# Weighted sums of three-block attention steps issued in one stretch of three blocks instead of two stretches

## The chip, the cores and the metric

The kernel runs on one core of one Trainium2 chip. The metric is the device time of one execution in microseconds (us). Its engines are PE (TensorE), DVE (VectorE), ACT (ScalarE), POOL (GpSimd) and SP (SyncE); each works through its own instructions in order, and they meet in semaphores.

## The reference

On x of 4 sequences of 1024 tokens and width 256, three layers run one after another: a mixture of experts, an attention, and the same mixture again.

```python
x = L0_attn_x
x = x + 0.5 * _L0_ffn_ref(_layernorm(x, axis=-1), Wg, W_in, W_out)
x = x + _L0_attn_ref(_layernorm(x, axis=-1), Wq, bq, Wk, bk, Wv, bv, Wo, bo, J_attn, lambda_attn)
x = x + 0.5 * _L0_ffn_ref(_layernorm(x, axis=-1), Wg, W_in, W_out)
```

The change lies in the attention alone, of 16 heads with 16 values each:

```python
scores = jnp.einsum('bhid,bhjd->bhij', Q, K) / scale
QJ = jnp.einsum('bhid,hde->bhie', jnp.tanh(Q), J_attn)
delta = jnp.einsum('bhie,bhje->bhij', QJ, jnp.tanh(K))
scores = scores + lambda_attn * delta
causal = jnp.triu(jnp.ones((S, S), dtype=bool), k=1)
scores = jnp.where(causal, -jnp.inf, scores)
probs = jax.nn.softmax(scores, axis=-1)
out = jnp.einsum('bhij,bhjd->bhid', probs, V)
```

## The kernel before

The attention takes 16 groups g of four heads (4 sequences by 4 groups of heads). Queries and keys are packed so that one product over 96 rows gives the whole score. For each query the kernel first needs the greatest score (the maximum pass, for a head that is more than one group ahead), then the exponentials of the scores less that maximum, then the weighted sums of the values.

**Six steps a group, four heads a step.** `STEPS` (line 1604) cuts the keys and queries of a group into six steps s. A step holds one to three blocks; a block is one tile of 128 keys against up to 512 queries. Step 0 has three blocks on the diagonal (512, 128 and 384 queries wide), step 1 one (256), steps 2 and 3 two full ones (512 each), step 4 three (512, 128, 384), step 5 one (256). For step s and head j, q = 4 s + j. In each q, PE forms the scores of one head of one step (`score`, line 2213) into one of two tiles `s_ps`, and ACT takes their exponential into `wts` (line 2089). The score of q needs the exponential of q - 2, which frees the tile.

**Masking on POOL.** Blocks on the diagonal have the weights above it set to zero by POOL (line 1913) after ACT has done all four heads of the step: three instructions for a three-block step, one for a one-block step, each for all four heads. PE waits for them on the semaphore `cleared`.

**Weighted sums.** `mix` (line 2225) multiplies the weights of a block by the values of its 128 keys. A product has 17 output rows (16 values and the sum of the weights), and the four heads go to four strips of the output tile `o_ps`, 32 partitions apart, so that four products use four strips of the array at once. The profile counts two matmuls for each such product: a block is 8 matmuls of the form `128*17`, in two sets of four. The sums of step s - 1 are issued among the scores of step s; those of step 5 at the end of the group. In `body` (line 2243), `when` (line 2256) says behind which heads j of step s they go: for a two-block step one block behind j = 1 and one behind j = 3; for a three-block step the first block behind j = 2 and the other two behind j = 3. The three-block steps are 0 and 4, so that concerns q = 6 and 7 (s = 1) and q = 22 and 23 (s = 5) of each group.

**The maximum pass, fitted in between.** In each q PE also issues two "maximum" units (`max_unit`, line 2177) of later heads: one ahead of the score of q, one behind it. A unit is one tile of 128 queries against up to 512 keys, written to one of three PSUM banks `m_ps`; DVE takes its maximum (lines 1964 and 1967). The twelve units of a head (`UNITS`, line 1608) are named here by query tile and half of the keys, as (6, 1). After the last, DVE folds them (line 1971), PE turns the result (`turn`, line 2193), ACT negates it (line 2032) and sends it to the packed queries. In the first ten groups (the hosts) PE also fits in the projections of later tokens, each into one of the same three banks: "x" transposes, "y" a product of six 512-wide matmuls for queries or keys, "v" one of six 256-wide matmuls for values. Of a host group, "y" comes at q = 5 and q = 6 (behind `mix`), and in groups with even numbers "v" at q = 21 and q = 23. In the last group, output tiles (line 295) take that place for q below 16.

**The order** is written out: `ORDER` and the assignment of banks (line 1712) are computed ahead from the units and projections alone. Before each one PE waits until the reader of the bank's earlier content is done (`free_bank`, line 2118). The bank of unit (7, 1), for instance, is in most groups the one that (5, 1) had. PE takes nothing past such a wait.

```python
when = {1: (3,), 2: (1, 3), 3: (2, 3)}[len(blocks)]
part = {j_: blocks[n:n + 1] if n + 1 < len(when) else blocks[n:] for n, j_ in enumerate(when)}.get(j)
if part:
    mix(g, u, s - 1, part, j == 3)
```

Of the kernel before, what the change touches and what calls it, by code (L numbers as in the profile page):

```python
# [1590 lines left out]
def attend(kit, c, proj, sum_dram, packs, v_dram, o_dram, inv_dram, wo_dram, bo_dram, group, group_in):  # L1591
# [18 lines left out]
    with ExitStack() as ctx:  # L1610
# [56 lines left out]
        def events(g, q):  # L1667

            first = PER_GROUP * (g + 1) + LEAD + sum(SHARE[:q])
            at = lambda units: after_units[min(units, len(after_units) - 1)]  # L1670
            return EVENTS[at(first):at(first + SHARE[q])]
# [16 lines left out]
        def project_at(g, q):  # L1688

            if g == GROUPS - 1:  # L1690
                return [("o", q)] if q < IN_ATTENTION else []
            what = IN_GROUP[g % 2].get(q) if 0 <= g < HOSTS else None
            return [what[:1] + (half_in(g),) + what[1:]] if what else []
# [418 lines left out]
        def tensor(pe):  # L2112
# [82 lines left out]
            def ahead(some):  # L2195
                for event in some:
                    if kind(event) == "turn":
                        turn(*event[:2])
                    elif kind(event) == "max":
                        max_unit(*event)  # L2200
                    else:
                        projected(event)
# [10 lines left out]
            def score(g, u, s, j):  # L2213
                ch, blocks = STEPS[s]
                q = s * GH + j
                if s == 0:
                    pe.wait_ge(row_in[j], (g + 1) * 16)
                pe.wait_ge(weighed, g * NS * GH + q + 1)
                for kt, col, q0, w, lead in blocks:
                    at = ch * QC + q0  # L2220
                    last = nc.tensor.matmul(s_ps[q % 2][:, col - lead:col + w], kp[u][:, j, kt * P:(kt + 1) * P],  # L2221
                                            qp[u][:, j, at - lead:at + w], start=True, stop=True)
                last.then_inc(scored, 1)

            def mix(g, u, s, blocks, done):

                ch = STEPS[s][0]
                if (g, s) == (0, 0):
                    pe.wait_ge(loaded[0], 16)
                for kt, col, q0, w, lead in blocks:  # L2230
                    if kt == 0:
                        pe.wait_ge(o_taken, 1 + g * 2 + ch)
                    if kt // 4 == ch:
                        pe.wait_ge(cleared, g * clears[NS] + clears[s + 1])
                    for j in range(GH):
                        pe.wait_ge(weighed, 2 + g * NS * GH + s * GH + j + 1)
                        last = nc.tensor.matmul(o_ps[j * HP:j * HP + HV, q0:q0 + w], vg[u][:, kt, j, :],  # L2237
                                                wts[(u * NS + s) % 2][:, j, col:col + w], start=(kt == 0),
                                                stop=(kt == ch * 4 + 2), skip_group_check=True)
                if done:  # L2240
                    last.then_inc(mixed, 1)

            def body(g, u):
                if g == 1:
                    pe.wait_ge(made, 2)
                for s in range(NS):
                    for j in range(GH):
                        q = s * GH + j
                        to_come = events(g, q)
                        ahead(to_come[:1])  # L2250
                        score(g, u, s, j)
                        ahead(to_come[1:2])
                        if s:

                            blocks = STEPS[s - 1][1]
                            when = {1: (3,), 2: (1, 3), 3: (2, 3)}[len(blocks)]
                            part = {j_: blocks[n:n + 1] if n + 1 < len(when) else blocks[n:] for n, j_ in enumerate(when)}.get(j)
                            if part:
                                mix(g, u, s - 1, part, j == 3)
                        ahead(to_come[2:])  # L2260
                        ahead(project_at(g, q))
                mix(g, u, NS - 1, STEPS[NS - 1][1], True)
# [3 lines left out]
            for event in LENT:  # L2266
                was_read(event)
            groups(body)

        functions = {"sync": sync, "gpsimd": gpsimd, "vector": vector, "scalar": scalar, "tensor": tensor}  # L2270
# [123 lines left out]
```

## Time and profile before

| | us |
|---|---|
| median of 3 runs | 1597.59 |
| lowest and highest run | 1595.5, 1605.68 |
| span of the profiled execution, first to last instruction | 1576.1 |
| PE busy | 1439.2 (91%) |
| DVE busy | 1022.7 (65%) |
| ACT busy | 712.3 (45%) |
| POOL busy | 684.3 (43%) |

The profile gives the span of its execution, and no time of its own beside it; the median is 21.5 us above that span. Mean granted TensorE clock over the span is 0.961 of full speed. The groups of the attention begin with their first score at 548.53 us and end at 1144.9 us; a group with an even number takes 41.3 us while it hosts projections, one with an odd number 37.4 to 37.5 us, and those from the tenth on about 32.1 us.

How to read the rows: times are us from the start of the span; a row of the timeline gives start, duration, engine, line, operation, tiles and count, and in brackets how long the engine was idle before it and what ended that. Matmuls overlap, so what one costs is the distance from its start to the start of the next, not its duration.

### The profile page before, as it was taken

How to read it: one execution, taken by the hardware profiler on the slowest of the kernel's cores; microseconds unless marked ns; L12 is line 12 of the kernel's file. 1: busy time of each engine (PE TensorE's matmuls, PEld its weight loads, DVE VectorE, ACT ScalarE, POOL GpSimd, SP SyncE). 2: the span in 40 equal slices, each digit the busy share in tenths (PEclk: the TensorE clock that was granted, in tenths of full speed). 3: DMA queues.
4: the chain of work that ended last, by engine and by line, in shares of the span. 5: the costliest groups of instructions: out<-in, count | busy, mean ns of one | idle time of the engine just before them, and what ended most of it. 6: DMA issues, size and time to landing. Idle time of an engine off the chain costs nothing. (4 is left out here: it accounts for less than half of the span.)

```text
span 1576.1 us, 25755 instructions
## 1 busy us (share of the span) xinstructions
PE 1439.2 (91%) x8992; PEld 1095.1 (69%) x8992; DVE 1022.7 (65%) x2609; ACT 712.3 (45%) x1117; POOL 684.3 (43%) x650
## 2 busy tenths in 40 slices
PE   4699999999877599999999999999986999999998
PEld 3589988989765355555555555555555888989997
DVE  7855665655386677776777778887367566565554
ACT  5333333333232156666666666666563333333332
POOL 1375556564524433333333331323403655656643
PEclk9799999999988699999999999999987999999999
DMA  9444443442378926666666668672064444345422
GB/s 307 131 106 98 94 88 64 92 101 28 67 216 201 316 76 169 168 169 169 169 168 169 154 169 242 161 218 100 29 204 148 101 96 87 67 94 101 93 37 25
DMA packets 125720, 208.61 MB, mean 132 GB/s; under 512 B 24424, under 2 KB 86376, under 8 KB 122536
## 3 DMA queue, kind: packets, MB, share of 16 engines
q1 hardware_dynamic: 88984, 160.06, 35.3%
q0 software_dynamic: 30720, 38.46, 14.9%
q10 hardware_dynamic: 5904, 8.66, 1.9%
q8 instruction: 63, 1.03, 0.3%
q14 instruction: 49, 0.40, 0.1%
HBM read 126.36 MB, written 84.64 MB: 134 GB/s over the span
## 5 line engine op out<-in xcount | busy, mean ns | idle before, releaser
L2089 ACT ACTIVATE a_wts<-a_s_psum 128x1024 f32<-128x1024 f32 (+1 forms) x384 | 301.0, 809 | 183.9 <-PE a_s_psum L2221 181.9
L1964 DVE CUSTOM_DVE_ANT_0 a_m_psum<-a_m_psum,mask 128x128 f32<-128x128 f32 (+1 forms) x492 | 238.7, 501 | 130.2 <-PE a_m_psum L2187 122.5
L2187 PE MATMUL a_m_psum<-a_kp,a_qp 96*128 96x512 f32 (+2 forms) x737 | 272.2, 398 | 20.5 <-DVE a_parts L1964 6.5
L2187 PEld LDWEIGHTS a_m_psum<-a_kp,a_qp 96*128 96x128 f32 x737 | 140.0, 192 | 130.1 <-DVE a_parts L1964 52.5
L1913 POOL TENSOR_SCALAR_AFFINE_SELECT a_wts<-a_wts 128x512 f32<-128x512 f32 x128 | 78.4, 637 | 328.0 <-ACT a_wts L2089 328.0
L1032 ACT ACTIVATE e_act_a<-e_a_psum 128x512 f32<-128x512 f32 (+1 forms) x192 | 101.2, 527 | 259.9 <-PE e_a_psum L1109 259.9
L2221 PE MATMUL a_s_psum<-a_qp,a_kp 97*128 97x512 f32 (+2 forms) x768 | 210.6, 356 | 0.4
L243 POOL DMA_INDIRECT e_slots<-normalized,e_token x160 | 168.7, 1054 | 81.7 <-issue 47.2
L949 DVE TENSOR_TENSOR e_hid<-e_act_a,e_g_psum 128x512 f32<-128x512 f32 (+1 forms) x192 | 114.5, 596 | 131.8 <-PE e_g_psum L1109 127.5
L1128 PE MATMUL e_o_psum<-e_w_hi,e_h_hi 128*128 128x256 f32 x640 | 183.2, 286 | 0.0
L890 POOL DMA_INDIRECT out<-e_res,e_sum_row x80 | 126.5, 1581 | 126.6 <-ACT e_res L1044 113.5
L890 POOL DMA_INDIRECT sums<-e_res,e_sum_row x80 | 126.5, 1581 | 126.1 <-ACT e_res L1044 105.2
L1128 PE MATMUL e_o_psum<-e_w_hi,e_h_lo 128*128 128x256 f32 x640 | 181.0, 283 | 0.0
L1128 PE MATMUL e_o_psum<-e_w_lo,e_h_hi 128*128 128x256 f32 x640 | 181.0, 283 | 0.0
L1967 DVE TENSOR_REDUCE a_parts<-a_m_psum 128x1 f32<-128x512 f32 x245 | 168.7, 689 | 8.5 <-PE a_m_psum L2187 6.2
L2237 PE MATMUL a_o_psum<-a_wts,a_vg 128*17 128x512 f32 (+3 forms) x1536 | 156.7, 496 | 4.3 <-POOL a_wts L1913 2.7
L2221 PEld LDWEIGHTS a_s_psum<-a_qp,a_kp 97*128 97x128 f32 x768 | 133.8, 192 | 18.4 <-ACT a_wts L2089 4.9
L1109 PE MATMUL e_a_psum<-e_s_hi,e_w_hi 128*128 128x512 f32 (+1 forms) x384 | 139.2, 363 | 5.4 <-DVE e_s_lo L929 2.8
L1044 ACT ACTIVATE e_res<-e_o_psum,e_gate 128x256 f32<-128x256 f32 x160 | 76.0, 475 | 147.3 <-PE e_o_psum L1128 147.3
L1109 PE MATMUL e_a_psum<-e_s_lo,e_w_hi 128*128 128x512 f32 (+1 forms) x384 | 136.0, 354 | 0.0
L1109 PE MATMUL e_a_psum<-e_s_hi,e_w_lo 128*128 128x512 f32 (+1 forms) x384 | 136.0, 354 | 0.0
L1109 PE MATMUL e_g_psum<-e_s_hi,e_w_hi 128*128 128x512 f32 (+1 forms) x384 | 135.9, 354 | 0.0
(292 smaller groups left out, 2757.3 us busy)
## 6 DMA issues: line engine op xcount, KB each, us to landing
packs<-x_res SPq DMA_DIRECT2D x48, 512.0 KB, 5.9
e_w_raw<-in_W_in SPq DMA_DIRECT2D x16, 1024.0 KB, 6.7
a_qp<-packs SPq DMA_DIRECT2D x15, 1024.0 KB, 8.1
a_kp<-packs SPq DMA_DIRECT2D x15, 1024.0 KB, 14.0
e_w_raw<-in_W_out SPq DMA_DIRECT2D x16, 512.0 KB, 8.6
normalized<-r_xn SPq DMA_DIRECT2D x16, 512.0 KB, 4.6
packs<-q_pack SPq DMA_DIRECT2D x16, 512.0 KB, 6.8
a_qp<-packs SPq DMA_DIRECT2D x16, 512.0 KB, 10.1
```

Of the source, the lines that this page charges most:

```text
L243: pool.indirect_dma_start(held["slots"][e % 2][:, j * ROW:(j + 1) * ROW], None, xn_dram, bass.IndirectOffsetOnAxis(ap=held["token"][:, at: ...
L890: nc.gpsimd.indirect_dma_start(sum_dram, bass.IndirectOffsetOnAxis(ap=sum_row[:, at:at + 1], axis=0), res[j][:], None, bounds_check=last_r ...
L949: nc.vector.tensor_tensor(hid[q][:, 0:n], act_a[q][:, 0:n], g_ps[q][:, 0:n], ALU.mult).then_inc(hid_done, 1)
L1032: nc.scalar.activation(act_a[q][:, 0:n], a_ps[q][:, 0:n], ACT.Gelu).then_inc(gelu_done, 1)
L1109: last = nc.tensor.matmul(bank[q][:, 0:n], w_in_at(w, k, half + f), s[:, k, c0:c0 + n], start=(z == 0), stop=(z == len(terms) - 1))
L1128: last = nc.tensor.matmul(o_ps[(u * ST + c0 // P + j) % 2][:, 0:D], s[:, k, j * P:(j + 1) * P], w_out_at(w, k), start=(z == 0), stop=(z == ...
L1964: nc.vector.tensor_tensor_reduce(products, products, c["mask"][:, QC - width:], 1.0, MASKED, ALU.add, ALU.max, top).then_inc(max_read, 1)
L1967: nc.vector.reduce_max(top, products, AX.X).then_inc(max_read, 1)
L2089: nc.scalar.activation(wts[(u * NS + s) % 2][:, j, 0:w], s_ps[q % 2][:, 0:w], ACT.Exp).then_inc(weighed, 1)
L2187: nc.tensor.matmul(m_ps[bank((n, h, z))][:, 0:stream], qp[n % NB][0:PACK, h, qt * P:(qt + 1) * P], kp[n % NB][0:PACK, h, part * QC:part * ...
L2221: last = nc.tensor.matmul(s_ps[q % 2][:, col - lead:col + w], kp[u][:, j, kt * P:(kt + 1) * P], qp[u][:, j, at - lead:at + w], start=True, ...
L2237: last = nc.tensor.matmul(o_ps[j * HP:j * HP + HV, q0:q0 + w], vg[u][:, kt, j, :], wts[(u * NS + s) % 2][:, j, col:col + w], start=(kt == ...
```

## The change

In `body` of the attention's tensor program, the entry for three blocks in `when` becomes `(3,)`. All three blocks of steps 0 and 4 are then issued behind head j = 3 of the next step; behind j = 2 there is none.

```diff
-                            when = {1: (3,), 2: (1, 3), 3: (2, 3)}[len(blocks)]
+                            when = {1: (3,), 2: (1, 3), 3: (3,)}[len(blocks)]
```

## Rows read from the trace of the kernel before

**Rows 1.** The page's costliest groups: the weighted sums.
```profile
L2237 PE MATMUL a_o_psum<-a_wts,a_vg 128*17 128x512 f32 (+3 forms) x1536 | 156.7, 496 | 4.3 <-POOL a_wts L1913 2.7
```

**Rows 2.** Busy time by window, one group each: 2, 4 and 11; the eighth number is the clock.
```profile
core 0: us, PE busy (x) PEld busy (x) DVE busy (x) ACT busy (x) POOL busy (x), PEclk, DMA share, GB/s
630.12:671.43 41.31, 38.95 (x239) 22.70 (x238) 29.23 (x90) 24.75 (x38) 14.03 (x18) 1.00 0.62 161
...
708.92:751.91 42.99, 40.61 (x239) 23.25 (x238) 29.21 (x89) 24.76 (x38) 14.02 (x18) 0.96 0.61 155
...
979.09:1011.24 32.15, 31.26 (x198) 17.10 (x197) 25.98 (x85) 20.44 (x31) 9.62 (x10) 1.00 0.57 157
```

**Rows 3.** Timeline of PE, q = 6 and 7 of host group 6.
```profile
799.60 0.40 PE L2187 MATMUL a_m_psum<-a_kp,a_qp 96*128 96x512 f32 x1
799.93 1.05 PE L2237 MATMUL a_o_psum<-a_wts,a_vg 128*17 128x512 f32 x8
800.92 0.50 PE L2143 MATMUL a_m_psum<-a_x_hi,q_w_hi 128*128 128x512 f32 x1
801.25 0.39 PE L2143 MATMUL a_m_psum<-a_x_lo,q_w_hi 128*128 128x512 f32 x1
801.48 0.40 PE L2143 MATMUL a_m_psum<-a_x_hi,q_w_lo 128*128 128x512 f32 x1
...
802.98 1.06 PE L2237 MATMUL a_o_psum<-a_wts,a_vg 128*17 128x128 f32 x16
```

**Rows 4.** Timeline of DVE there: the end of reading unit (0, 0).
```profile
800.04 0.14 DVE L1964 DVE_READ_ACCUMULATOR2_ANT a_parts<- 128x1 f32 x1
```

**Rows 5.** Timeline of PE, q = 6 and 7 of group 11.
```profile
985.38 0.49 PE L2187 MATMUL a_m_psum<-a_kp,a_qp 96*128 96x512 f32 x1
986.07 1.05 PE L2237 MATMUL a_o_psum<-a_wts,a_vg 128*17 128x512 f32 x8 [0.20 <-issue]
...
987.72 1.06 PE L2237 MATMUL a_o_psum<-a_wts,a_vg 128*17 128x128 f32 x16
988.70 0.27 PE L2193 MATMUL a_m_psum<-ident,a_tops 128*8 128x128 f32 x1
```

**Rows 6.** Timeline of DVE there: ends of reading (6, 1) and (0, 0).
```profile
985.18 0.14 DVE L1964 DVE_READ_ACCUMULATOR2_ANT a_parts<- 128x1 f32 x1
...
986.61 0.14 DVE L1964 DVE_READ_ACCUMULATOR2_ANT a_parts<- 128x1 f32 x1
```

**Rows 7.** Timeline of PE, q = 22, q = 23 and the group's end, even host group 6.
```profile
826.03 1.05 PE L2237 MATMUL a_o_psum<-a_wts,a_vg 128*17 128x512 f32 x8
...
827.74 1.06 PE L2237 MATMUL a_o_psum<-a_wts,a_vg 128*17 128x128 f32 x16
...
829.63 0.63 PE L2237 MATMUL a_o_psum<-a_wts,a_vg 128*17 128x256 f32 x8
830.18 0.39 PE L2187 MATMUL a_m_psum<-a_kp,a_qp 96*128 96x256 f32 x1
```

**Rows 8.** Timeline of DVE there: reading (5, 1), then (7, 0).
```profile
826.42 0.14 DVE L1964 DVE_READ_ACCUMULATOR2_ANT a_parts<- 128x1 f32 x1
826.42 0.69 DVE L1967 TENSOR_REDUCE a_parts<-a_m_psum 128x1 f32<-128x512 f32 x1
```

**Rows 9.** Timeline of PE, the end of odd host group 7.
```profile
865.91 1.74 PE L2237 MATMUL a_o_psum<-a_wts,a_vg 128*17 128x128 f32 x24
867.58 0.38 PE L2187 MATMUL a_m_psum<-a_kp,a_qp 96*128 96x256 f32 x1
```

**Rows 10.** Timeline of DVE there: reading (6, 0), then the end of (5, 1).
```profile
863.57 0.69 DVE L1967 TENSOR_REDUCE a_parts<-a_m_psum 128x1 f32<-128x512 f32 x1
...
864.51 0.14 DVE L1964 DVE_READ_ACCUMULATOR2_ANT a_parts<- 128x1 f32 x1
```

**Rows 11.** Timeline of PE, q = 22 and the group's end, group 14.
```profile
1104.47 1.05 PE L2237 MATMUL a_o_psum<-a_wts,a_vg 128*17 128x512 f32 x8 [1.20 <-POOL a_wts L1913]
...
1107.11 0.62 PE L2237 MATMUL a_o_psum<-a_wts,a_vg 128*17 128x256 f32 x8 [0.29 <-POOL a_wts L1913]
```

## The prediction

> **What bounds the kernel now.** I read the list of costliest groups first, then busy time by window, then the timelines of PE and DVE around q = 6, 7, 22 and 23. The weighted sums take 156.7 us of PE and are hardly waited for: 4.3 us in 1536 matmuls [rows 1]. PE is busy in 31.26 of 32.15 us of a late group, DVE in 25.98, ACT in 20.44 [rows 2]. So PE sets the time, and an attention of 16 groups would gain from whatever makes PE's stream shorter. But DVE, at 81%, runs close behind, and PE reaches it only through three banks. Where PE issues several units with little between them it waits for DVE; a block of weighted sums is the time in which DVE catches up. The change takes one such block from between the units of q = 6 and 7 (and 22 and 23) and puts it behind them all. So the question at each of the 32 places (16 groups, two each) is what PE meets once that block is gone.
>
> **Prices, from starts to starts.** A 512-wide matmul among others like it costs 0.23 (801.25 to 801.48) [rows 3]. From the last unit to the sums it is 0.33 (799.60 to 799.93): going in costs 0.10. A stretch of one 512-wide block takes 0.99 (799.93 to 800.92) [rows 3], one of a 256-wide block 0.55 (829.63 to 830.18) [rows 7]; so 256 columns cost 0.44, and 0.11 is paid once, at the end. The two blocks of 128 and 384 take 0.98 together (987.72 to 988.70) [rows 5]: the number of blocks costs nothing, their columns do. Behind the stretch the first matmul costs 0.33 instead of 0.23 (800.92 to 801.25) [rows 3], another 0.10. One stretch less therefore saves 0.10 + 0.11 + 0.10 = 0.31 us of PE, and 32 of them 9.9 us. The first block, moved into the later stretch, costs 0.88 there.
>
> That PE pays for going in and out is what the rows show. The Trainium skill has it as a rule (TensorEngine Tiling (Array Packing), Key Properties): a change of tiling mode drains the engine. By the rule alone the change is a gain wherever it acts, which is the first rival below.
>
> **Where PE goes instead.** A unit starts 0.06 after its bank's reader ends: DVE ends reading (6, 1) at 985.18 + 0.14 = 985.32 [rows 6], the unit that waits starts at 985.38 [rows 5]. I replay each kind of place with that, up to the start of the sums of the 128-wide block, which both orders have. DVE's own times are kept where it is busy or fed earlier than now.
>
> - **s = 1, host groups (10 places).** Without the block, "y" could start 0.23 behind the unit of 799.60, but it takes the bank of (0, 0), which DVE has read only at 800.18 [rows 4]. So "y" starts at 800.24 instead of 800.92 [rows 3], 0.68 earlier. The stretch starts as much before 802.98, at 802.30; with the first block's 0.88 the 128-wide block starts at 803.18. That is **0.20 later** than now: +2.0.
> - **s = 1, groups 10 to 14 (5 places).** No projection lies between. Unit (1, 0) and the score of q = 7 go earlier, but (4, 0) needs the bank of (0, 0), read until 986.61 + 0.14 = 986.75 [rows 6]. It starts at 986.81, the stretch 0.33 later at 987.14, the 128-wide block at 988.02 instead of 987.72 [rows 5]: **0.30 later**, +1.5. That PE no longer waits there for POOL (0.20 of idle) [rows 5] is in this already.
> - **s = 5, even host groups (5 places).** Unit (6, 1) has the bank of (5, 1), read until 826.56; (7, 1) that of (7, 0), read until 826.42 + 0.69 = 827.11 [rows 8]. It starts at 827.17, the stretch at 827.50, the 128-wide block at 828.38 instead of 827.74 [rows 7]: **0.64 later**, +3.2. Here DVE also had a "v" to read at that point, so it is furthest behind.
> - **s = 5, odd host groups and 10 to 13 (9 places).** Unit (6, 1) waits for its bank until 863.57 + 0.69 = 864.26, (7, 1) until 864.51 + 0.14 = 864.65 [rows 10], so the stretch starts at 864.71 + 0.33 = 865.04 and the 128-wide block at 865.92 instead of 865.91 [rows 9]: nothing gained. But the sums of step 5 follow in the same stretch, 24 matmuls in 1.67 us [rows 9], where 768 columns and the way out take 3 x 0.44 + 0.11 = 1.43. The other 0.24 is the wait for POOL's mask of step 5, which follows the last exponential. That exponential now comes some 0.8 earlier, and the wait goes: **0.23 earlier**, -2.1.
> - **s = 5, groups 14 and 15 (2 places).** No units are left, and PE waits 1.20 for POOL before the first block [rows 11]. That stays at 1104.47; the last score goes into this wait. Three blocks of 1024 columns then end at 1104.47 + 4 x 0.44 = 1106.23, and step 5's sums start there instead of at 1107.11, their own wait of 0.29 gone [rows 11]: 0.88 earlier each, -1.8.
> - **s = 1, group 15 (1 place).** No units either: the 0.31 of a stretch, -0.3.
>
> ACT gets the scores of q = 7 and 23 earlier and has nothing to lose; POOL the same. No DMA is moved. The turn behind q = 7, ACT's negation, and the exponential of q = 8 come behind the stretch in their queues, so a place that is late hands its delay on. I see nothing between a place and the next that would absorb it, since DVE too has run dry by the end of the long stretch.
>
> **Sum.** 2.0 + 1.5 + 3.2 - 2.1 - 1.8 - 0.3 = **+2.5 us**, so a span of 1576.1 + 2.5 = 1578.6 and, the median standing 21.5 above that span, a time of **1600.1 us**. What the trace doesn't show is how DVE runs once it is fed earlier. From below, no wait at any place is a saving of 9.9 + 2.1 for POOL's waits + about 1.2 more at groups 14 and 15: -13. From above, every place as bad as the worst, 32 x 0.64 = +20. I take the replay, whose places stand on their own rows; an error of 0.15 a place is 5 us. Its own range is 1594 to 1606, the three runs before themselves having 1595.5 to 1605.7.
>
> **Rivals.**
> - **The switches are saved and nothing waits** (0.09). For it: PE is the bound, and at the ends of [rows 7] and [rows 5] DVE is idle in the long stretch. Against: at four of the six kinds of place the bank's reader ends after the time at which PE would want it. It gives 1597.6 - 13 = 1585. This is also the page's rule taken by itself.
> - **The clock falls more often** (0.04), the case on the other side. PE idles up to 0.6 in front of (6, 1) where it was busy with sums. In group 4 the granted clock was 0.96 over the group and its time 42.99, against 41.31 in group 2 at 1.00 [rows 2]: an episode at the lower of the two levels, 1.2 instead of 2.4 GHz, costs 1.7 us. Its place would be the five even groups, behind q = 22, and perhaps the late ones at q = 6. From 9 more episodes it is over 1% with the +2.5; 12 give 1597.6 + 2.5 + 20 = 1620. The Trainium skill warns of it (TensorE: Matmul & The Clock Gate, on psum-queue depth-cycling): short idle times between bursts make the gate fall and rise. Against it: group 2 has the same order and waits as group 4 and kept its clock.
> - **DVE is further behind than the replay has it** (0.05): (7, 1) or (4, 0) late by a further read of 0.69 at all places. It gives up to +20, 1618, and decides beyond 16.
> - **The change does nothing on PE** (0.01): `part` with one entry in `when` takes all blocks, so no.
>
> The forecast itself has 0.81.
>
> **How the numbers follow.** A change can be told here from about 1%, 16 us. The forecast and the saved switches lie within that; the other two reach it about half the time: faster 0.02, same 0.92, slower 0.06. The range takes the forecast's own and reaches toward the saved switches, without holding them whole, since 0.09 lies there, and a little above 1606: 1588 to 1607.
>
> **What would show it.** Right: groups of 37.4 become 37.4 + 0.20 - 0.23, even host groups 41.3 become 42.1, late ones 32.2; a stretch of 24 matmuls behind q = 7 and of 32 behind q = 23 (24 where "v" follows); at q = 23 of even groups PE idle some 0.6 for line 1964. Wrong: even groups at or under 41.3, which would say that DVE reads ahead; or a clock under 1.00 in more than the one group.

## The result and the profile after

The changed kernel has a median of 1610.55 us (1601.4 to 1617.21, 20 runs), the kernel before, measured beside it in 20 runs, one of 1603.66. The ratio is **1.0049 (1.0031 to 1.0068)**: slower by 7.9 us in the mean (6.9 between the medians), and clear of noise. The prediction gave +2.5 us and a chance of 0.92 that the change stays within 1%. It does, but it is three times as large as forecast, and the time lies outside the range of 1588 to 1607. Part of that is the base: 1597.59 on the three runs shown ahead, 1603.66 on twenty. Of the 10.5 us between 1600.1 and 1610.55, 6.1 are this shift, which no step of the prediction is to blame for; 7.9 on the base shown ahead would have been 1605.5.

The profiled execution of the changed kernel has a span of 1601.1 us and a time of 1603.19, 2.1 above it, and in all other runs here it stands as far above. By that the profile shown ahead, with its span of 1576.1, is of an execution of about 1578 us, faster than any of the twenty runs of the kernel before. Most of the 25 us between the two spans has nothing to do with the change: the attention starts 9.5 us later (first score at 558.1 instead of 548.5), in code that is the same, and what follows the attention is longer by about as much. So I compare stretches of the attention. From its first score to its last sums it went from 596.3 to 603.2 us, and a second profile of the changed kernel, of a shorter execution (span 1583.3), has 603.0. These are windows of the changed kernel: groups 1 to 9, 10 to 14, then groups 8, 2, 3, 13 and 11 alone. The first number is the length, the one behind POOL the granted clock.

```profile
601.44:960.48 359.04, 338.14 (x2035) 197.56 (x2034) 257.61 (x798) 216.35 (x324) 125.98 (x162) 0.99 0.64 165
960.48:1126.75 166.27, 159.71 (x970) 86.36 (x968) 125.77 (x403) 101.75 (x151) 49.68 (x51) 0.97 0.58 171
880.83:923.04 42.21, 39.08 (x240) 22.93 (x238) 29.29 (x90) 24.71 (x38) 14.02 (x18) 1.00 0.56 145
...
639.15:681.34 42.19, 39.07 (x240) 22.92 (x238) 29.30 (x90) 24.72 (x38) 14.01 (x18) 1.00 0.61 157
681.34:718.78 37.44, 35.72 (x219) 20.76 (x218) 28.35 (x90) 23.49 (x36) 13.99 (x18) 1.00 0.68 177
...
1062.07:1094.49 32.42, 31.29 (x199) 17.43 (x198) 25.84 (x85) 20.42 (x31) 11.50 (x11) 1.00 0.55 157
992.89:1026.70 33.81, 32.70 (x199) 17.81 (x197) 25.78 (x85) 20.39 (x31) 9.54 (x10) 0.95 0.53 150
```

The same stretches of the kernel before:

```profile
592.47:946.95 354.48, 337.32 (x2035) 193.53 (x2034) 257.81 (x798) 216.63 (x324) 126.15 (x162) 1.00 0.64 167
946.95:1108.12 161.17, 155.09 (x969) 83.60 (x968) 126.67 (x403) 101.85 (x151) 49.08 (x51) 1.00 0.60 176
```

Two things are to be seen. Where the clock is 1.00, an even host group is 0.9 longer than before (42.2 against 41.3 [rows 2]), an odd one is unchanged (37.44), and a late one 0.26 longer (32.42 against 32.15 [rows 2]). And group 11 has a clock of 0.95 and takes 1.4 more than its clean neighbour. The kernel before has one episode at half clock in groups 1 to 14 (group 4 [rows 2]); the changed one has five: groups 4 and 6 as hosts, and 11, 12 and 14, where before there was none. (Group 12 takes 33.58 us in the kernel before too, at full clock; the 32.1 said ahead of late groups doesn't hold for it.)

**A late group without an episode**, q = 6 and 7 of group 10, PE and then DVE of the changed kernel:

```profile
966.79 0.50 PE L2187 MATMUL a_m_psum<-a_kp,a_qp 96*128 96x512 f32 x1
967.44 0.39 PE L2187 MATMUL a_m_psum<-a_kp,a_qp 96*128 96x256 f32 x1 [0.15 <-DVE a_parts L1964]
967.67 0.28 PE L2221 MATMUL a_s_psum<-a_qp,a_kp 97*128 97x256 f32 x1
968.22 0.49 PE L2187 MATMUL a_m_psum<-a_kp,a_qp 96*128 96x512 f32 x1 [0.27 <-DVE a_parts L1964]
968.65 1.92 PE L2237 MATMUL a_o_psum<-a_wts,a_vg 128*17 128x512 f32 x24
970.49 0.27 PE L2193 MATMUL a_m_psum<-ident,a_tops 128*8 128x128 f32 x1
```

```profile
967.81 0.30 DVE L1964 CUSTOM_DVE_ANT_0 a_m_psum<-a_m_psum,mask 128x128 f32<-128x128 f32 x1 [0.21 <-DVE a_tops L1971]
968.02 0.14 DVE L1964 DVE_READ_ACCUMULATOR2_ANT a_parts<- 128x1 f32 x1
```

This answers to [rows 5, 6]. The sums are one stretch of 24 matmuls. Unit (4, 0), at 968.22, starts 0.06 after DVE has read (0, 0), at 968.02 + 0.14, as the replay had it. New is that from (4, 0) to the sums it is 0.43 (968.22 to 968.65) and not 0.33. The 0.10 goes with the wait, not with the sums: in group 8 below, (6, 1) with 384 columns takes 0.28 behind a wait (918.17 to 918.45), where 512 columns without one take 0.23 [rows 3].

**The same place with the clock down**, group 11:

```profile
999.17 1.03 PE L2187 MATMUL a_m_psum<-a_kp,a_qp 96*128 96x512 f32 x2
1000.04 0.28 PE L2221 MATMUL a_s_psum<-a_qp,a_kp 97*128 97x256 f32 x1
1000.60 0.80 PE L2187 MATMUL a_m_psum<-a_kp,a_qp 96*128 96x512 f32 x1 [0.28 <-DVE a_parts L1964]
1001.33 3.05 PE L2237 MATMUL a_o_psum<-a_wts,a_vg 128*17 128x512 f32 x24
```

The order and the waits are those of group 10. The clock falls at 1000.26, ahead of (4, 0), and from there on matmuls run at 1.2 instead of 2.4 GHz; the stretch takes 3.05 instead of 1.92.

**The end of an even host group**, q = 22 on of group 8:

```profile
917.26 0.39 PE L2187 MATMUL a_m_psum<-a_kp,a_qp 96*128 96x512 f32 x1
918.17 0.44 PE L2187 MATMUL a_m_psum<-a_kp,a_qp 96*128 96x384 f32 x1 [0.52 <-DVE a_parts L1964]
918.45 0.28 PE L2221 MATMUL a_s_psum<-a_qp,a_kp 97*128 97x256 f32 x1
918.72 0.49 PE L2187 MATMUL a_m_psum<-a_kp,a_qp 96*128 96x512 f32 x1
919.14 1.92 PE L2237 MATMUL a_o_psum<-a_wts,a_vg 128*17 128x512 f32 x24
```

Where a block of sums stood before [rows 7], PE now waits 0.52 for line 1964 ahead of unit (6, 1), as forecast.

### The profile page after: what moved, and what is told of

Read it like the earlier page. It is cut to its first block and busy times, and to the rows that moved or that the text cites. A ratio compares the mean times of both kernels' runs of the same rounds, so it can differ in the third digit from the quotient of the medians.

```text
span 1601.1 us, 25753 instructions
## 1 busy us (share of the span) xinstructions
PE 1450.4 (91%) x8990; PEld 1107.6 (69%) x8992; DVE 1021.2 (64%) x2609; ACT 711.2 (44%) x1117; POOL 697.6 (44%) x650
## 5 line engine op out<-in xcount | busy, mean ns | idle before, releaser
L2187 PEld LDWEIGHTS a_m_psum<-a_kp,a_qp 96*128 96x128 f32 x737 | 139.8, 192 | 126.4 <-DVE a_parts L1964 41.3
L890 POOL DMA_INDIRECT out<-e_res,e_sum_row x80 | 135.6, 1695 | 121.8 <-ACT e_res L1044 106.8
L890 POOL DMA_INDIRECT sums<-e_res,e_sum_row x80 | 132.0, 1649 | 126.3 <-ACT e_res L1044 103.1
L2237 PE MATMUL a_o_psum<-a_wts,a_vg 128*17 128x512 f32 (+3 forms) x1536 | 150.7, 501 | 1.1 <-POOL a_wts L1913 1.1
```

The lines of the kernel that those rows point to most:

```text
L890: nc.gpsimd.indirect_dma_start(sum_dram, bass.IndirectOffsetOnAxis(ap=sum_row[:, at:at + 1], axis=0), res[j][:], None, bounds_check=last_r ...
L2187: nc.tensor.matmul(m_ps[bank((n, h, z))][:, 0:stream], qp[n % NB][0:PACK, h, qt * P:(qt + 1) * P], kp[n % NB][0:PACK, h, part * QC:part * ...
```

## Experiments

Two theories. **A**: the block of sums between the units was the time in which DVE emptied the banks; without it PE meets a late bank at most places, and what a stretch less saves is lost there. **B**: the gaps so made bring the granted clock down. Rivals: chance, or a long stretch being bad in itself. All ratios are to the kernel before, run beside the others of its set on the same chip; its own median was 1603.66, 1589.07, 1578.5 and 1577.95 us in the four sets, so times of different sets aren't compared. "Groups 10 to 14" is the time from the first score of group 10 to that of group 15, in the one profiled execution.

For the clock there is more than one profile each: every run on record has its mean granted clock over the whole span. Beside each kernel stands the kernel before in the same set:

| kernel (runs) | mean granted clock | the kernel before (runs) |
|---|---|---|
| step 0 alone in one stretch (10) | 0.9547 | 0.9586 (27) |
| step 4 alone (10) | 0.9561 | 0.9586 |
| changed, with dummy matmuls (10) | 0.9585 | 0.9586 |
| all behind q = 6 (6) | 0.9573 | 0.9586 |
| before, short reads (4) | 0.9652 | 0.9599 (8) |
| changed, short reads (4) | 0.9652 | 0.9599 |
| changed, projection moved (4) | 0.9557 | 0.9599 |
| step 4 alone, projection moved (5) | 0.9584 | 0.9599 |
| changed, once more (6) | 0.9578 | 0.9615 (23) |
| picked places (12) | 0.9618 | 0.9615 |
| picked places, with dummies (12) | 0.9617 | 0.9615 |

Differences of ten runs to the kernel before are good to 0.001 or so, those of four to 0.0015. A fall of 0.001 over 1590 us is 1.6 us of lost clock, about one episode.

### One step at a time

```diff
-  3: (3,)}[len(blocks)]
+  3: (3,) if s == 1 else (2, 3)}[len(blocks)]     # only step 0, behind q = 7
```

> Only step 0 (sums behind q = 7) in one stretch; step 4 as before. Theory A (a late bank at each place, as the timeline of the changed kernel shows it): q = 5 to 7 of an odd host group take 7.45 us instead of 7.28, q = 6 and 7 of a late group 4.52 instead of 4.15; q = 22 and 23 as before (4.41 in late and odd groups, 5.18 in even ones). Theory B (the granted clock falls in the gaps in front of the stretch): the four added episodes at half clock in the changed kernel all lay in q = 5 to 7, so three to five episodes remain in the attention, at 1.2 to 1.7 us each, and the attention takes 596.3 + 1.7 + 1.9 + 4 to 7 = 604 to 607 us from first score to last sums. Rival (the clock has nothing to do with these gaps): at most one episode and about 600 us.

Measured: 1.0052 (1.0024 to 1.0081). Groups 10 to 14, windows of this kernel and, behind it, of the one with only step 4 below:

```profile
955.17:1123.23 168.06, 160.75 (x970) 85.65 (x968) 126.12 (x403) 101.84 (x151) 48.93 (x51) 0.97 0.58 169
```

```profile
957.85:1119.10 161.25, 155.89 (x970) 85.12 (x969) 126.42 (x403) 101.85 (x151) 49.93 (x51) 0.99 0.62 176
```

With step 0 alone the episodes of groups 11, 12 and 14 are all there, and a place that is clean takes what was said: 7.45 and 5.42 us for q = 5 to 7 of odd and late groups. The attention took 604.9, within the 604 to 607 of theory B, and over all runs the clock is 0.0039 lower than the kernel before's.

```diff
-  3: (3,)}[len(blocks)]
+  3: (3,) if s == 5 else (2, 3)}[len(blocks)]     # only step 4, behind q = 23
```

> Only step 4 (sums behind q = 23) in one stretch; step 0 as before. Theory A: q = 22 and 23 take 5.9 us instead of 5.18 in even host groups, 4.26 instead of 4.42 in odd and late ones, groups 14 and 15 gain 0.9 each; together 3.6 - 1.4 - 1.8 = +0.4. Theory B: no episode beyond the one or two that the kernel before has, so the attention takes 596 to 598 us and the time is that of the kernel before within its interval. Rival (each gap of 0.6 us in the even groups brings the clock down): two or more episodes near q = 22, and over 599 us.

Measured: 1.0024 (0.9993 to 1.0054), no difference that can be told. q = 22 and 23 take 5.90 in even groups, 4.27 in odd and late ones, as expected. But the attention took 602.1 and not 596 to 598: there were episodes in groups 4 and 8 at q = 5 and in group 14 at q = 6, a longer one in group 0, and one at the end, as the kernel before has. None lay near q = 22 of an even group, so the rival's account fails; that even groups lose the clock at q = 5 happens with and without the change (group 4 [rows 2]).

So step 0 alone has a loss as large as the whole one. Step 4 alone may have none; the intervals of the two overlap. Its clock is 0.0025 lower than the kernel before's, and whether that is the change the ten runs don't settle.

### Dummy matmuls in the gaps

```diff
+  def fill(g, q, n):
+      pe.wait_ge(weighed, g * NS * GH + q + 1)
+      keep_running(nc.tensor, c, s_ps[q % 2][:, QC:QC + P], n)
...
+  if s == 1 and j == 3 and HOSTS <= g < GROUPS - 1: fill(g, q, 3)   # ahead of (1, 0)
   ahead(to_come[:1])
   score(g, u, s, j)
+  if s == 1 and j == 3 and HOSTS <= g < GROUPS - 1: fill(g, q, 2)   # ahead of (4, 0)
   ahead(to_come[1:2])
+  if s == 1 and j == 2 and g < HOSTS: fill(g, q, 3)                 # ahead of "y"
```

> The changed kernel with dummy matmuls (128 wide, identity by identity, into the unused half of the score tile, read by nobody) where PE waits for a bank at s = 1: three behind the second unit of q = 6 in host groups, three ahead of the first unit and two behind the score of q = 7 in groups 10 to 14. Theory B: places take what they took in the changed kernel (7.45 in odd hosts, 4.52 in late groups, within 0.1), but the episodes at half clock in q = 5 to 7 of groups 6, 11, 12 and 14 go, so the attention is 3 to 6 us shorter than the changed kernel's 603.2. Rival (episodes are chance, or come from the waits ahead of q = 6): as many episodes as in the changed kernel and no gain, or a loss of up to 15 x 0.2 = 3 us from the dummies.

Measured: 1.0034 (1.0009 to 1.0059). The timeline of PE at q = 6 and 7 of group 11 with them:

```profile
997.83 0.83 PE L1270 MATMUL a_s_psum<-ident 128*128 128x128 f32 x6
998.42 0.36 PE L2187 MATMUL a_m_psum<-a_kp,a_qp 96*128 96x256 f32 x1
998.62 0.28 PE L2221 MATMUL a_s_psum<-a_qp,a_kp 97*128 97x256 f32 x1
998.74 0.61 PE L1270 MATMUL a_s_psum<-ident 128*128 128x128 f32 x4
999.11 0.48 PE L2187 MATMUL a_m_psum<-a_kp,a_qp 96*128 96x512 f32 x1
999.52 1.92 PE L2241 MATMUL a_o_psum<-a_wts,a_vg 128*17 128x512 f32 x24
```

The window of its groups 10 to 14:

```profile
958.61:1121.03 162.42, 157.95 (x1020) 90.76 (x1019) 125.73 (x403) 101.76 (x151) 49.80 (x51) 1.00 0.59 175
```

Groups 10 to 14 have a clock of 1.00 and take 162.4 instead of 166.3, though the dummies make each clean place 0.17 longer: each is two records, and three take 0.59, more than the gap. That is theory B for the late groups. In the hosts one episode was left (group 2, q = 5) and nothing was gained, 359.7 us against 359.0. The attention as a whole took 603.5 us, not 3 to 6 less than 603.2: group 0 took 3.5 more, in a longer stretch at half clock from its q = 2 on, where there are no dummies. Between the whole kernels 1.0034 and 1.0049 can't be told apart. The clock can: over the ten runs it is that of the kernel before (0.9585 against 0.9586), where step 0 alone has 0.9547. What is left of the loss, at an unchanged clock, is the late banks and the dummies themselves.

### The stretch behind q = 6 instead of q = 7

```diff
-  3: (3,)}[len(blocks)]
+  3: (2,)}[len(blocks)]
...
-  mix(g, u, s - 1, part, j == 3)
+  mix(g, u, s - 1, part, j == when[-1])
```

> All three blocks in one stretch behind q = 6 (q = 22) instead of q = 7 (q = 23). As many stretches as in the changed kernel. Theory A (what costs is that units stand close together without a block between them): now the units of q = 7, 8 and 9 stand without a block, with DVE having run dry in the long stretch, and at q = 6 the stretch waits for POOL's mask, 0.2 to 0.4 in late groups; places should gain up to 0.31 each against the kernel before where the banks at q = 7 are free, so the attention takes 588 to 597 us. Rival (a long stretch is bad by itself, since DVE, starved in it, hands its delay on): as slow as the changed kernel, 600 us or more.

Measured: 1.0109 (1.0074 to 1.0144), the slowest of its set, and the opposite of what I had expected: the attention took 617.8 us, which is the rival's side of the forecast. The clock has little part in it. Groups 10 to 14 keep it, and take 167.1 us where the kernel before takes 161.2:

```profile
968.03:1135.17 167.14, 154.77 (x969) 84.80 (x968) 126.66 (x403) 101.63 (x151) 49.09 (x51) 1.00 0.58 170
```

The timeline of PE behind the stretch, q = 7 and 8 of group 7, shows why:

```profile
858.25 0.28 PE L2187 MATMUL a_m_psum<-a_kp,a_qp 96*128 96x256 f32 x1
858.37 0.28 PE L2221 MATMUL a_s_psum<-a_qp,a_kp 97*128 97x256 f32 x1
858.49 0.39 PE L2187 MATMUL a_m_psum<-a_kp,a_qp 96*128 96x512 f32 x1
859.36 0.27 PE L2193 MATMUL a_m_psum<-ident,a_tops 128*8 128x128 f32 x1 [0.48 <-DVE a_parts L1964]
859.82 0.44 PE L2187 MATMUL a_m_psum<-a_kp,a_qp 96*128 96x384 f32 x1 [0.18 <-DVE a_parts L1967]
```

The turn needs the bank of (1, 0), the next unit that of (4, 0), and DVE has only just been given both. There is nothing of sums to cover that. q = 7 takes 1.96 us, as it does in the kernel before with two blocks of sums in it. I read it as theory A at another place; what excludes the rival, a long stretch being bad in itself, is the next experiment and the picked places. That DVE is idle when a stretch ends helps nothing if the units behind it follow each other bare. My expectation had kept the banks' order in mind and not the time a read takes after it.

### DVE made quick

```diff
-  top, products = parts[h % 2][:, qt, part:part + 1], m_ps[at][:, 0:width]
+  top, products = parts[h % 2][:, qt, part:part + 1], m_ps[at][:, width - P:width]
...
-  c["mask"][:, QC - width:]
+  c["mask"][:, QC - P:]
```

On the kernel before:

> The kernel before, with DVE reading only the last 128 columns of each unit of the maximum pass (the rest is left out of the maximum, PE's products are unchanged). It is the base of the next kernel. Reads fall from 0.5 to 0.7 us to about 0.3, so PE should hardly wait for banks: late groups from 32.15 to about 31, the whole attention 10 to 25 us shorter than 596. By the rival that the banks are not what PE waits for, no more than 3 us.

On the changed kernel:

> The changed kernel with the same short reads on DVE. If late banks are the whole reason why a stretch less gains nothing (theory A), then here the change gains what switches cost: 0.31 a place, late and odd groups each 0.5 to 0.6 us shorter than in the kernel above, groups 1 to 14 together some 8 to 9 us shorter, and no added episode of half clock in the late groups. Rival (one long stretch costs as much as two, or hands on a delay by itself): groups within 0.2 us of those of the kernel above.

Measured: 0.9835 (0.9809 to 0.9860) and 0.9800 (0.9775 to 0.9825), medians 1552.63 and 1545.64, with four runs each that don't overlap. **The sign turns**: with short reads a stretch less makes the kernel 7.0 us faster, where with the real reads it makes it 7.9 slower. The clock isn't what turns it, at 0.9652 in both. Windows of groups 10 to 14 and of group 8, of the first and then of the second:

```profile
926.26:1085.72 159.46, 153.04 (x969) 84.51 (x968) 77.50 (x403) 101.44 (x151) 49.01 (x51) 0.98 0.61 178
850.59:890.60 40.01, 37.61 (x239) 22.60 (x238) 18.09 (x90) 24.50 (x38) 13.99 (x18) 1.00 0.60 153
```

```profile
925.05:1077.66 152.61, 149.30 (x969) 85.51 (x968) 77.55 (x403) 101.44 (x151) 49.85 (x51) 1.00 0.66 186
849.04:889.59 40.55, 37.53 (x239) 22.82 (x238) 18.08 (x89) 24.51 (x38) 14.05 (x18) 1.00 0.58 151
```

DVE is busy in half of the time, the changed order has no episode in the attention at all, and late groups gain 0.9 (31.5 to 30.6). But not all of A's forecast holds. The gain in groups 1 to 14 was 5.9 and not 8 to 9, and some 2.6 of it are two episodes, in groups 11 and 14, that the first of the two profiles has and the second hasn't. By kinds of place, in clean groups, the change is worth:

| place | real reads | short reads |
|---|---|---|
| step 0, hosts | +0.17 | +0.17 |
| step 0, late groups | +0.39 | -0.39 |
| step 4, even hosts | +0.71 | +0.32 |
| step 4, odd hosts and late groups | -0.15 | -0.43 |

Step 4 is as theory A has it. In odd and late groups no wait for a bank is left in q = 21 to 23, and the place gains what a stretch costs and a little more; in even ones a wait of 0.38 is left in place of 0.52.

In the hosts at step 0 nothing changes. "y" waits for the bank of (0, 0), whose read was 128 columns wide in either kernel. Here are the matmul of (0, 0), the end of its read and "y", in group 8 of the changed order with short reads:

```profile
858.42 0.29 PE L2188 MATMUL a_m_psum<-a_kp,a_qp 96*128 96x256 f32 x1
859.10 0.14 DVE L1965 DVE_READ_ACCUMULATOR2_ANT a_parts<- 128x1 f32 x1
859.29 0.50 PE L2144 MATMUL a_m_psum<-a_x_hi,q_w_hi 128*128 128x512 f32 x1 [0.24 <-DVE a_parts L1965]
```

That wait is the delay from PE's matmul to the end of DVE's read, 0.8 us (858.42 to 859.24), and no shorter read removes it.

The gain at step 0 in late groups has another source. q = 6 of group 10, the first block in the kernel before with short reads and POOL's mask there; then (4, 0) and the long stretch in the changed order:

```profile
933.06 1.05 PE L2238 MATMUL a_o_psum<-a_wts,a_vg 128*17 128x512 f32 x8 [0.93 <-issue]
931.15 1.81 POOL L1913 TENSOR_SCALAR_AFFINE_SELECT a_wts<-a_wts 128x512 f32<-128x512 f32 x3 [6.08 <-ACT a_wts L2090]
```

```profile
931.84 0.50 PE L2188 MATMUL a_m_psum<-a_kp,a_qp 96*128 96x512 f32 x1 [0.28 <-DVE a_parts L1965]
932.27 1.92 PE L2238 MATMUL a_o_psum<-a_wts,a_vg 128*17 128x512 f32 x24
```

(4, 0) waits 0.28 as before, for the same bank of (0, 0). But PE, freed of its waits for longer reads, comes to the first block so early that it stands idle for 0.93 us until POOL has ended the mask at 932.96. The changed order has no block there and doesn't meet that wait. So at these places the experiment swaps one limit for another, and the turn of the sign there isn't proof of theory A; the proof is in step 4.

### The value projection moved into the gap

```diff
-  18: ("v", 0), 21: ("v", 1), 23: ("v", 2)}
+  18: ("v", 0), 22: ("v", 1), 23: ("v", 2)}
```

> The changed kernel with the value projection of even host groups at q = 22 instead of q = 21, where the sums' block was. Theory A: its six matmuls fill PE's wait for (6, 1), and DVE's add for it no longer stands ahead of the read of (5, 1). q = 21 to 23 take 6.9 to 7.1 us instead of 7.66 in the changed kernel (6.94 before), even groups without an episode 41.4 to 41.7 instead of 42.2. Rival (what costs is the long stretch behind q = 23): 7.66 stays.

> A version meant to beat both: step 4 in one stretch, step 0 in two as before, the value projection at q = 22 in even host groups. From the timelines: odd and late groups 0.15 shorter than before (9 places), groups 14 and 15 0.9 each, even groups as before: -3.2 us, 0.2%, at most 2 episodes in the attention. Rival: something else moves with the projection and it is no faster than with step 4 alone, 1.002.

Measured: 1.0119 (1.0096 to 1.0142) with both steps in one stretch, 1.0059 (1.0038 to 1.0081) with step 4 alone. The place did what was said: q = 21 to 23 of even groups take 6.96 us, and an even group 41.5. But the banks of all that follows are dealt out anew. In odd hosts q = 7 takes 3.7 instead of 2.8, and in the first of the two kernels the clock fell at q = 1 or 2 of groups 3, 5 and 9 and in groups 11 to 14. Its groups 1 to 9 took 368.2 instead of 359.0. A gain worked out at one place of an order that is dealt out in a row is no gain of the kernel. At q = 7 of odd hosts the assignment now gives (4, 0) the bank of (1, 0), the unit just ahead of it, so PE waits for the whole of its read. Both units in group 7:

```profile
848.00 0.29 PE L2187 MATMUL a_m_psum<-a_kp,a_qp 96*128 96x256 f32 x1
849.02 0.51 PE L2187 MATMUL a_m_psum<-a_kp,a_qp 96*128 96x512 f32 x1 [0.62 <-DVE a_parts L1964]
```

### The places that gain, alone

```diff
+  whole = s == 5 and (g % 2 == 1 or g >= HOSTS)
-  3: (3,)}[len(blocks)]
+  3: (3,) if whole else (2, 3)}[len(blocks)]
```

> A version made from the places that gained: one stretch only for step 4 and only in odd host groups and from group 10 on (11 places); all else as in the kernel before. Theory A: q = 22 and 23 take 4.27 instead of 4.42 in nine groups and 0.9 less in groups 14 and 15, -3.2 us; no gap that brings the clock down is added, so one to three episodes as in the kernel before. Ratio 0.996 to 1.000. Rival (placement of the stretches has effects elsewhere, such as in the next group): 1.002 or more.

The same with dummies ahead of "y" at q = 5 of even hosts, `fill(g, q, 4)`:

> The version above with four dummy matmuls (128 wide, into the unused half of the score tile) in even host groups ahead of the query product of q = 5, where PE idles 0.6 us and where the kernel before has its episode at half clock. Theory B: no episode in q = 5 and 6 of the even groups, where the other kernels' profiles have one or two at 1.6 us; 0 to 3 us less than the version above, ratio 0.994 to 0.999. Rival: as many episodes, and 0.1 to 0.2 us lost at each of the five places.

And beside them the changed kernel once more:

> The changed kernel once more, beside the two versions below. If the falls of the clock follow from the places and not from chance, the profile again has episodes at q = 7 in two to four of the groups 10 to 14, where the kernel before had none; groups without one as in the first profile (37.4, 42.2, 32.4). Ratio to the kernel before 1.002 to 1.008. Rival (chance): no episode or one in groups 10 to 14.

Measured beside each other: the changed kernel 1.0053 (1.0032 to 1.0074); the picked places **0.9971 (0.9958 to 0.9984)**, faster than both; with dummies 0.9977 (0.9960 to 0.9995). The picked kernel's q = 22 and 23 take 4.27 at its places, groups 14 and 15 gain as in the changed kernel (an episode at q = 23 hides it in group 14 of this profile), and the other groups are the kernel before's. With dummies groups 1 to 14 have no episode (352.13 and 159.70 us, against 353.74 and 161.31 in the picked one, which had two). That is one execution: over the twelve runs of each the clock is 0.9617 and 0.9618, and the times don't differ. So the dummies in even groups gave nothing, and theory B's forecast for q = 5 fails.

The changed kernel's second profile repeats its first:

```profile
592.80:951.98 359.18, 338.26 (x2035) 197.51 (x2034) 257.80 (x798) 216.67 (x324) 126.21 (x162) 0.99 0.63 165
951.98:1118.07 166.09, 159.75 (x969) 86.38 (x968) 125.89 (x403) 101.81 (x151) 49.75 (x51) 0.97 0.59 171
```

Again the clock fell in groups 11, 12 and 14, and not in 10 and 13. So it did in all three profiles with step 0 in one stretch behind q = 7, the real reads, no projection moved and no dummies; in the kernel before and in the picked one never at q = 6 or 7 of these groups. It can fall there without the change: the kernel with step 4 alone had one episode at q = 6 of group 14, the kernel before with short reads one at q = 6 of group 11. But three groups out of five in each of three profiles, and a clock that is 0.0037 and 0.0039 lower over sixteen runs, are not chance. Why 10 and 13 are spared, with the same order and the same waits, the runs don't show.

## Why the prediction was wrong

**The mechanism of the sum was right and nearly its size.** By kinds of place, predicted and measured, from the distances between scores in clean groups: step 0 in host groups +0.20, measured +0.17 (7.28 to 7.45 for q = 5 to 7); in late groups +0.30, +0.39 (5.02 to 5.41), the difference being the 0.10 that a unit costs more behind a wait; step 4 in even hosts +0.64, +0.71 (5.18 to 5.89); in odd and late groups -0.23, -0.15; in group 14 -0.88, -0.92. So each kind of place was replayed to within 0.1. By places the change costs 5 x 0.88 in even hosts, 5 x 0.02 in odd ones, 4 x 0.24 in groups 10 to 13, -0.53 in group 14 and, by the same prices, about -1.2 in group 15: **+3.7 us**, against +2.5 predicted. Late banks are what costs: in step 4, where short reads remove the wait, a place gains 0.43.

**The step that failed is the clock**, a term that the sum put at nothing. I made it a rival of 0.04, with the objection that "group 2 has the same order and waits as group 4 and kept its clock", and put it down for the even groups behind q = 22, "and perhaps the late ones at q = 6". It happened in late groups, in three of five, at q = 6 or 7, in both profiles of the change; and at q = 22 of even groups never. An episode costs 1.4 to 1.7: q = 5 to 7 takes 6.85, 6.99 and 7.10 in groups 11, 12 and 14 against 5.41 in a clean one. The three are 4.7 us.

The two profiles can be added up. Groups 1 to 14 went from 515.7 to 525.3 us, +9.7. Places are 4.0 of that (four even groups, the late ones and group 14), four added episodes 5.9 (group 6 with 1.2, and the three late ones); the two make 9.9. Groups 0 and 15 went the other way, -0.6 and -2.2: each had an episode in the profile before and none in the one after, so part of what the change seems to gain in group 15 is luck of the profile. Together +6.9 for the attention. The mean clock of the six further runs says the same without that luck: 0.0037 lower than the kernel before beside them, on 1584 us, is 5.9 us, more than half of the loss. Places and clock so taken give 3.7 + 5.9 = 9.6 us, against 7.9 and 8.3 measured in the two sets; the clock's part is known to some 2 us only.

What misled me is that I priced the clock as something that either doesn't happen or is so frequent that it decides over 1%. I counted from nine more episodes, while three would already have carried the forecast's +2.5 to about +7. A rare and dear event belongs into the sum as count times price, even if only a few are likely. The rows to see it were there: q = 6 and 7 of late groups had short waits already [rows 5, 6], the block of sums was the dense part between them, and the replay itself had PE standing still ahead of (4, 0).

**The first rival**, the saved switches, also had a true price: where short reads leave no wait, at step 4 of odd and late groups, a stretch less gains 0.43, the 0.31 worked out and a little of POOL's mask. Its condition, banks that are free in time, doesn't hold here. The rival of DVE further behind than replayed is excluded by the places above. The range was lopsided: it reached 12 us down for a rival of 0.09 and only 7 up, where the two on the slower side were and where the base then moved by 6.

## What to carry to other kernels

Where one engine hands tiles to another through few banks, other work between the hand-overs is not idle cost of switching: it is the time in which the reader catches up. Gathering such work saves the switch and exposes the reads; replay the next two or three hand-overs with the reader's own end times before counting a switch as saved, and apply the change only at the places where the bank is free anyway. And count new gaps in front of matmuls twice, once as time and once as a risk for the clock, with the price of an episode taken from the same trace.

## What the runs showed of the hardware

The granted clock fell although no gap was long: in the 3 us ahead of the fall at 1000.26 in group 11 PE stood idle for 0.11 and 0.15 us and a few hundredths beside, and the wait of 0.28 in the timeline above came when the clock was down already. Five dummies at such a place kept it at 1.00. The Trainium skill says as much of another kernel (TensorE: Matmul & The Clock Gate, A second HAM failure mode: psum-queue depth-cycling): short idle times between groups of matmuls suffice to make the gate fall and rise. The trace agrees in that waits for PSUM banks, none of them long, stand ahead of the falls. That they suffice it doesn't show: groups 10 and 13 have the same ones and kept their clock, and so did all five late groups of the changed order with short reads, with 0.13 and 0.28 at q = 7.

A stretch of column-tiled products costs 0.31 us for going in and out; a matmul that had to wait costs 0.10 more than one that didn't, whatever follows it. Within a stretch time goes by columns and not by the number of blocks, 0.44 per 256 columns for four heads at once.
